# Delta net: products with V of both value heads interleaved over the four quarters of TensorE's array

## Chip, core and metric

One Trainium2 chip, one of its cores. The metric is the device time of the whole kernel in microseconds (us). The engines are called as the profile calls them: PE (TensorE's matmuls), PEld (its weight loads), DVE (VectorE), ACT (ScalarE), POOL (GpSimd) and SP (the queue that issues the DMAs).

## What is computed

A small perceiver-like model of six residual layers on x of 16 x 64 x 256 in float32: latent cross attention, attention, a feed-forward layer, a second cross attention, a gated delta net (`_L1_attn_ref`), and a mixture of experts. Only the delta net is touched. Cut to its core:

```
mixed = silu(conv4(hidden @ W_qkv.T))        # q, k: 16 heads of 128; v: 32 heads of 128
q, k = repeat(q, 2), repeat(k, 2)            # two value heads share one key head
q, k = l2norm(q) * DK**-0.5, l2norm(k)
g, beta = -exp(A_log) * softplus(a + dt_bias), sigmoid(b)
def step(state, (qt, kt, vt, gt, bt)):       # over the 64 positions
    state = state * exp(gt)
    delta = (vt - kt @ state) * bt
    state = state + outer(kt, delta)
    return state, qt @ state
o = rmsnorm(outs) * norm_w * silu(z)
y = o @ W_out.T
```

## The kernel before

Tokens lie as (2 batches x 64 positions) on 128 partitions, 8 such tiles (`TILES`). The delta net runs a loop over the 16 key heads; each brings two value heads (`hv` 0 and 1). The recurrence is written as matrices of 64 x 64 per batch and value head: `AT` (what is to be inverted), `T` (the inverse), `PT` (scores with decays), their product mixed, `Ms`, and then `Ms` times `V`. Since one batch needs 64 rows and 64 columns only, each product of this kind uses one quarter of the 128 x 128 array: batch 0 rows and columns 0 to 63, batch 1 rows and columns 64 to 127. The other two quarters are not used by them.

The order on every engine is written by hand in a function `step(j)` for that engine, and the engines meet at semaphores. In step j the kernel finishes head j while it projects and prepares head h = j + 1 (its convolution, its scores, its `AT`) and projects the output of head g = j - 1. These parts carry names that the prediction uses:

- `cross(j, 4)` on PE is the first use of `T` of head j. It waits for the DMAs that bring the inverted 16 x 16 blocks into `T` and `TT16` (the trace calls the wait "DMA TT<-t_blocks").
- After it PE runs two projections (`project`), `grow`, `scores(h)`, `turn_T`, `cross(j, 5)`, `grow(j, 5)` and the first projection of z (`project_z(j, 0)`). ACT takes tanh of that (`tanh_z`, tile `thz`), DVE multiplies (`silu_z`, tile `z2`), and only behind it in DVE's order stands `make_A(h, .)`, which writes `AT` of head h.
- SP waits for `AT` (`blocks_out(h)`), writes it to DRAM (`a_rows`), reads the blocks on the diagonal back as `sy`; POOL inverts them in 30 small dependent steps (`substitute`, tiles `tm`, `ti`); SP writes the result (`t_blocks`) and reads it back into `T` and `TT16` (`blocks_in`). That ends in `cross(h, 4)` of the next step.
- Meanwhile PE runs `mix(j, hv)` (T times PT into banks 4 and 5), DVE scales it to `Ms` (`keep_M`, with `sk`, one factor for each row), PE runs `project_z` 2 and 3, `outs(j, hv)` (`Ms` times `V` into banks 6, 7 for head 0 and 4, 5 for head 1), and then the output projection `project_out(g, .)`, `turn_v(h, 0)`, and the beginning of the next step, up to `cross(h, 4)`.
- `square_o` on ACT, and `gate`, `sum_o` and then `residual(g, .)` on DVE take up the results. `residual(g, 0)` frees banks 2 and 3, on which `turn_v(h, 0)` waits.
- `keep_v(h, hv)` on ACT copies `V` of one value head from PSUM into SBUF.

Of the kernel before, what the change touches and what calls it, by code (L numbers as in the profile page):

```python
# [6 lines left out]
ALU = mybir.AluOpType  # L7
ACT = mybir.ActivationFunctionType
AX = mybir.AxisListType

P = 128
B, S, D = 16, 64, 256
TILES = B * S // P
# [880 lines left out]
def phase3(nc, d, sb, semaphores, C, over, each, X, HT, PS, carrier):  # L894
# [9 lines left out]
    with ExitStack() as ctx:  # L904
        ga = sb(ctx, "ga", [P, TILES, 2 * HV])

        with ExitStack() as c2:
# [5 lines left out]
            s = semaphores(c2, "ab_in ab_mm ab_v ab_a")  # L913
            av, bv = ab[:, :, 0:HV], ab[:, :, HV:2 * HV]
            ea, eb = e[:, :, 0:HV], e[:, :, HV:2 * HV]
            with nc.Block() as block:
# [36 lines left out]
                def _(a):  # L953
# [23 lines left out]
        wo = sb(ctx, "wo", [P, 2, D])  # L977
# [15 lines left out]
        rr = sb(ctx, "rr", [P, 2, 2 * TILES])  # L993
        r2 = sb(ctx, "r2", [P, 2, 2 * TILES])
        sk = sb(ctx, "sk", [P, 2, TILES])
        dd = sb(ctx, "dd", [P, 2, TILES])
        AT = sb(ctx, "AT", [P, 2, 2, TILES, S])
        PT = sb(ctx, "PT", [P, 2, 2, TILES, S])
# [3 lines left out]
        T = sb(ctx, "T", [P, 2, TILES, S])  # L1002
# [3 lines left out]
        Ms = sb(ctx, "Ms", [P, 2, TILES, S])  # L1006
        V = sb(ctx, "V", [P, 2, TILES, DK])
        dl = sb(ctx, "dl", [P, 2, TILES, DK])
        ms = sb(ctx, "ms", [P, 2, TILES])
        s = semaphores(ctx, "win vin zin cin oin nin nws pj tap conv th y zz zt z2 qq kk dg nr nm rr gj gm dps e ed et av pd "  # L1010
                            "d1 sin sub d3 t16 tt tts x xs yy tu mt mss o us ms gz fz og0 og1 ogt ogs wo xa wof vt vc zero", "p3_")
        NQ = 8
        NS = 2 * SUB
        QB = (0, 1, 0, 1, 0, 1, 0, 0)
# [3 lines left out]
        def wide(b0):  # L1018
            return PS[:, b0:b0 + 2, :].rearrange("p k n -> p (k n)")

        def bank(k):
            return PS[:, k, :].rearrange("p (n s) -> p n s", s=S)
# [4 lines left out]
        def obank(hv):  # L1027
            return 6 if hv == 0 else 4
# [16 lines left out]
        def flat(ap):  # L1045
            return ap.rearrange("p n c -> p (n c)")

        with nc.Block() as block:
# [91 lines left out]
            def _(pe):  # L1140
# [81 lines left out]
                        mm = pe.transpose(PS[:, 2 + n // 4, (n % 4) * P:(n % 4 + 1) * P], y[:, 2 + hv, n * P:(n + 1) * P], C("ident"))  # L1222
                    mm.then_inc(s["vt"], 1)

                def each_batch(b0, lhs, rhs):

                    w = rhs.shape[2]
                    for n in range(TILES):
                        for b in range(2):
                            r = slice(64 * b, 64 * b + S)  # L1230
                            at = n * w
                            mm = pe.matmul(PS[r, b0 + at // 512, at % 512:at % 512 + w], lhs[r, n, :], rhs[r, n, :], start=True, stop=True)
                    return mm

                def turn_T(j, hv):
                    if hv == 0:
                        pe.wait_ge(s["tu"], j * 2 + 1)
# [41 lines left out]
                def mix(j, hv):  # L1279
                    if hv == 0:  # L1280
                        pe.wait_ge(s["tu"], j * 2 + 2)
                    pe.wait_ge(s["pd"], j * 2 + hv + 1)
                    each_batch(4 + hv, T[:, hv, :, :], PT[:, j % 2, hv, :, :]).then_inc(s["mt"], 1)

                def outs(j, hv):
                    pe.wait_ge(s["mss"], j * 2 + hv + 1)
                    pe.wait_ge(s["vc"], j * 2 + hv + 1)
                    each_batch(obank(hv), Ms[:, hv, :, :], V[:, hv, :, :]).then_inc(s["o"], 1)

                def turn_out(g, hv):  # L1290
                    pe.wait_ge(s[f"og{hv}"], g + 1)
# [29 lines left out]
                def step(j):  # L1321
                    h, g = j + 1, j - 1
                    beside, tail = h < HK, g >= 0
                    if beside:
                        project(h, 0)
                    turn_v(j, 1)
                    if beside:
                        project(h, 1)
                        decay_sums(h)
                        project(h, 2)  # L1330
                    if tail:
                        turn_out(g, 0)
                    if beside:
                        project(h, 3)
                    if tail:
                        turn_out(g, 1)
                    cross(j, 4)
                    if beside:
                        project(h, 4)
                    grow(j, 4)  # L1340
                    if beside:
                        project(h, 5)
                        scores(h)
                    turn_T(j, 0)
                    turn_T(j, 1)
                    cross(j, 5)
                    if beside:
                        project(h, 6)
                    grow(j, 5)
                    project_z(j, 0)  # L1350
                    if beside:
                        project(h, 7)
                    project_z(j, 1)
                    for hv in range(2):
                        mix(j, hv)
                    project_z(j, 2)
                    project_z(j, 3)
                    for hv in range(2):
                        outs(j, hv)
                    if tail:  # L1360
                        for m in range(4):
                            project_out(g, m)
                    if beside:
                        turn_v(h, 0)
# [15 lines left out]
            def _(a):  # L1380
                def tap(h, q):
                    c, f = q // 2, q % 2
                    if q == 0:
                        a.wait_ge(s["cin"], h * 16 + 16)
                    a.wait_ge(s["pj"], h * NQ + q + 1)
                    if h * NQ + q >= 2:
                        a.wait_ge(s["y"], h * NQ + q - 1)
                    a.activation(acc[:, f, :], PS[:, QB[q], :], ACT.Copy, scale=wc[:, h % 2, 4 * c + 3:4 * c + 4]).then_inc(s["tap"], 1)  # L1388

                def tanh(h, q):  # L1390
                    a.wait_ge(s["conv"], h * 24 + q * 3 + 3)
                    a.activation(th[:, q % 2, :], acc[:, q % 2, :], ACT.Tanh, scale=0.5).then_inc(s["th"], 1)  # L1392

                def tanh_z(j, m):
                    a.wait_ge(s["zz"], j * 4 + m + 1)
                    if j * 4 + m >= 2:
                        a.wait_ge(s["z2"], j * 4 + m - 1)
                    a.activation(thz[:, m % 2, :], PS[:, ZB[m], :], ACT.Tanh, scale=0.5).then_inc(s["zt"], 1)
# [27 lines left out]
                def keep_v(h, hv):  # L1426
                    a.wait_ge(s["vt"], h * 2 + hv + 1)
                    if h > 0:
                        a.wait_ge(s["o"], h * 2 - 2 + hv + 1)
                    a.activation(flat(V[:, hv, :, :]), wide(2), ACT.Copy).then_inc(s["vc"], 1)  # L1430

                def scale_wo(g):
                    a.wait_ge(s["oin"], g * 16 + 16)
# [8 lines left out]
                def step(j):  # L1442
                    h, g = j + 1, j - 1
                    beside, tail = h < HK, g >= 0
                    if beside:
                        tap(h, 0)
                    keep_v(j, 1)
                    if beside:
                        tap(h, 1)
                        tanh(h, 0)  # L1450
                        decays(h)
                        tap(h, 2)
                        tanh(h, 1)
                    if tail:
                        keep_out(g, 0)
                    if beside:
                        tap(h, 3)
                        tanh(h, 2)
                    if tail:
                        keep_out(g, 1)  # L1460
                    keep_X(j, 4)
                    if beside:
                        tanh(h, 3)
                        tap(h, 4)
                        tap(h, 5)
                        tanh(h, 4)
                    for hv in range(2):
                        keep_TT(j, hv)
                    if beside:
                        tanh(h, 5)  # L1470
                    keep_X(j, 5)
                    if tail:
                        scale_wo(g)
                    if beside:
                        tap(h, 6)
                        tanh(h, 6)
                    tanh_z(j, 0)
                    if beside:
                        tap(h, 7)
                    tanh_z(j, 1)  # L1480
                    if beside:
                        tanh(h, 7)
                    tanh_z(j, 2)
                    tanh_z(j, 3)
                    for hv in range(2):
                        square_o(j, hv)
                    if beside:
                        keep_v(h, 0)
# [4 lines left out]
                for q in range(NQ):  # L1493
                    tap(0, q)
                    if q == 3:
                        decays(0)
                    tanh(0, q)
                keep_v(0, 0)
                for j in range(HK):
                    step(j)  # L1500
                scale_wo(LAST)
# [91 lines left out]
            def _(v):  # L1593
# [56 lines left out]

                def keep_M(j, hv):
                    v.wait_ge(s["mt"], j * 2 + hv + 1)
                    v.tensor_tensor(Ms[:, hv, :, :], bank(4 + hv), each(sk[:, j % 2, :], S), ALU.mult).then_inc(s["mss"], 1)

                def residual(g, m):
                    v.wait_ge(s["wo"], g * 2 + m + 1)
# [298 lines left out]
```

## Time and profile before

| | |
|---|---|
| median of 3 runs | 1953.88 us (1947.71 to 1959.5) |
| the profiled execution: its own time / its span | 1954.76 us / 1952.6 us |
| mean granted clock of TensorE | 0.941 |
| the delta net's loop over heads | about 694 to 1643 us of the span |
| PE, POOL, DVE, ACT busy in the span | 88%, 28%, 60%, 31% |

The span is the time from the first to the last instruction; the profiled execution's own time has 2.2 us around it. A value of 1.00 in the column PEclk stands for the array at 2.4 GHz, 0.50 for 1.2 GHz; a value between them is a mean over a stretch that held both.

### The profile page before, as it was taken

How to read it: one execution, taken by the hardware profiler on the slowest of the kernel's cores; microseconds unless marked ns; L12 is line 12 of the kernel's file. 1: busy time of each engine (PE TensorE's matmuls, PEld its weight loads, DVE VectorE, ACT ScalarE, POOL GpSimd, SP SyncE). 2: the span in 40 equal slices, each digit the busy share in tenths (PEclk: the TensorE clock that was granted, in tenths of full speed). 3: DMA queues.
4: the chain of work that ended last, by engine and by line, in shares of the span. 5: the costliest groups of instructions: out<-in, count | busy, mean ns of one | idle time of the engine just before them, and what ended most of it. 6: DMA issues, size and time to landing. Idle time of an engine off the chain costs nothing. (4 is left out here: it accounts for less than half of the span.)

```text
span 1952.6 us, 34931 instructions
## 1 busy us (share of the span) xinstructions
PE 1719.2 (88%) x14360; PEld 1174.4 (60%) x14360; DVE 1164.5 (60%) x1853; ACT 600.8 (31%) x997; POOL 552.0 (28%) x890
## 2 busy tenths in 40 slices
PE   3899968998995548999999999999999877999998
PEld 1333336886784226766776777766677665556555
DVE  4555557678764537676777767776677613443432
ACT  1111114334422313343444333433433311212212
POOL 1100014113211045444445554453554321000000
PEclk9899978999997869999999999998999978999999
DMA  6221120010000111111122111211211113200000
GB/s 200 84 59 47 49 52 1 1 33 12 1 1 3 33 30 31 43 37 39 37 48 47 39 42 36 48 41 35 47 36 43 26 23 113 87 0 0 0 0 21
DMA packets 150907, 74.47 MB, mean 38 GB/s; under 512 B 128176, under 2 KB 131504, under 8 KB 149488
## 3 DMA queue, kind: packets, MB, share of 16 engines
q1 hardware_dynamic: 150768, 72.48, 14.5%
q8 instruction: 104, 1.70, 0.4%
q14 instruction: 35, 0.29, 0.1%
HBM read 54.62 MB, written 17.83 MB: 37 GB/s over the span
## 5 line engine op out<-in xcount | busy, mean ns | idle before, releaser
L1604 DVE SCALAR_TENSOR_TENSOR acc<-PS,wc,acc 128x504 f32<-128x504 f32 (+2 forms) x384 | 281.5, 733 | 104.7 <-ACT acc L1388 95.5
L1158 PE MATMUL PS<-HT,wv 128*128 128x512 f32 x256 | 140.5, 676 | 8.3 <-DVE acc L1604 8.3
L1528 POOL TENSOR_TENSOR rr<-nm,con 128x16 f32<-128x16 f32 x16 | 46.4, 2901 | 341.1 <-DVE nm L1632 341.1
L1175 PE MATMUL PS<-wz,HT 128*128 128x256 f32 x512 | 123.6, 390 | 18.4 <-DVE acc L1604 17.0
L1388 ACT ACTIVATE acc<-PS,wc 128x512 f32<-128x512 f32 x128 | 87.7, 685 | 168.0 <-PE PS L1158 119.3
L1158 PE MATMUL PS<-HT,wkq 128*128 128x512 f32 x256 | 125.1, 614 | 11.4 <-DMA wkq<-in_gdn_w 8.5
L1614 DVE SCALAR_TENSOR_TENSOR y<-th,acc 128x512 f32<-128x512 f32 x128 | 93.3, 729 | 60.6 <-ACT th L1392 60.4
L1175 PEld LDWEIGHTS PS<-wz,HT 128*128 128x128 f32 x512 | 95.1, 192 | 40.8 <-DVE acc L1604 19.0
L1316 PE MATMUL PS<-wo,ogT 128*128 128x256 f32 x512 | 116.9, 387 | 1.1 <-ACT ogT L1440 1.1
L298 PE MATMUL PS<-HT,cw 128*96 128x512 f32 x256 | 117.5, 613 | 0.0
L1392 ACT ACTIVATE th<-acc 128x512 f32<-128x512 f32 x128 | 80.2, 626 | 116.8 <-DVE acc L1604 116.6
L1260 PE MATMUL PS<-T,AT 64*64 64x32 f32 x2048 | 74.5, 232 | 43.7 <-DMA TT<-t_blocks 43.7
L1316 PEld LDWEIGHTS PS<-wo,ogT 128*128 128x128 f32 x512 | 97.6, 193 | 17.0 <-issue 2.6
L1260 PEld LDWEIGHTS PS<-T,AT 64*64 64x64 f32 x2048 | 71.7, 150 | 48.2 <-DMA TT<-t_blocks 48.0
L1790 PE MATMUL PS<-wg,hT 128*128 128x512 f32 x192 | 97.1, 631 | 0.6 <-DMA wu<-in_moe_u 0.3
L1808 PE MATMUL PS<-wd,acT 128*128 128x256 f32 x384 | 90.3, 382 | 2.2 <-ACT acT L1831 2.2
L1790 PE MATMUL PS<-wu,hT 128*128 128x512 f32 x192 | 90.3, 593 | 0.0
L1556 POOL TENSOR_TENSOR tm<-sy,ti 128x15 f32<-128x15 f32 (+7 forms) x240 | 63.8, 266 | 93.2 <-DMA sy<-a_rows 75.7
L298 PEld LDWEIGHTS PS<-HT,cw 128*96 128x96 f32 x256 | 41.6, 168 | 76.0 <-issue 76.0
L1877 DVE SCALAR_TENSOR_TENSOR act<-th,PS 128x512 f32<-128x512 f32 x48 | 33.0, 687 | 90.6 <-ACT th L1827 90.6
L1275 PEld LDWEIGHTS PS<-Xs,TT 64*64 64x64 f32 x2048 | 67.3, 144 | 29.3 <-issue 15.9
L370 DVE TENSOR_TENSOR ra<-PS,con 96x512 f32<-96x512 f32 x32 | 21.8, 683 | 101.7 <-PE PS L298 101.7
(228 smaller groups left out, 3357.6 us busy)
## 6 DMA issues: line engine op xcount, KB each, us to landing
a_rows<-AT SPq DMA_DIRECT2D x16, 512.0 KB, 2.6
wk<-in_l0x_k SPq DMA_DIRECT2D x16, 384.0 KB, 3.3
queries_scratch<-tts SPq DMA_DIRECT2D x32, 128.0 KB, 2.7
b<-queries_scratch SPq DMA_DIRECT2D x8, 512.0 KB, 5.0
wkq<-in_gdn_w SPq DMA_DIRECT2D x16, 256.0 KB, 3.2
wv<-in_gdn_w SPq DMA_DIRECT2D x16, 256.0 KB, 2.8
wz<-in_gdn_w SPq DMA_DIRECT2D x16, 256.0 KB, 2.9
wo<-in_gdn_w SPq DMA_DIRECT2D x16, 256.0 KB, 2.6
```

The source lines that it names most:

```text
L298: mm = pe.matmul(PS[0:HQ, 2 + 2 * f + c, :], cw[:, p, k, c * HQ:(c + 1) * HQ], HT[:, k, f * 512:(f + 1) * 512], start=(k == 0), stop=(k == ...
L1158: mm = pe.matmul(PS[:, QB[q], :], w[:, o:o + DK], HT[:, k, f * 512:(f + 1) * 512], start=(k == 0), stop=(k == DC - 1))
L1175: mm = pe.matmul(PS[:, ZB[m], w * 256:(w + 1) * 256], HT[:, k, n * P:(n + 1) * P], wz[:, k * 2 * DK:(k + 1) * 2 * DK], start=(k == 0), sto ...
L1260: mm = pe.matmul(PS[r, 6, m * 2 * SUB:(m + 1) * 2 * SUB], matrices(AT[r, j % 2, :, :, :])[:, m, :], cols, start=True, stop=True)
L1275: mm = pe.matmul(PS[r, 7, m * 2 * SUB:(m + 1) * 2 * SUB], matrices(turned[r, :, :, :])[:, m, :], Xs[r, m, :], start=True, stop=True)
L1316: mm = pe.matmul(PS[:, wbank(m), w * D:(w + 1) * D], ogT[:, hv, n * P:(n + 1) * P], wo[:, hv, :], start=(hv == 0), stop=(hv == 1))
L1388: a.activation(acc[:, f, :], PS[:, QB[q], :], ACT.Copy, scale=wc[:, h % 2, 4 * c + 3:4 * c + 4]).then_inc(s["tap"], 1)
L1392: a.activation(th[:, q % 2, :], acc[:, q % 2, :], ACT.Tanh, scale=0.5).then_inc(s["th"], 1)
L1604: v.scalar_tensor_tensor(a0, p0, wc[:, h % 2, 4 * c + 2 - k:4 * c + 3 - k], a0, ALU.mult, ALU.add).then_inc(s["conv"], 1)
L1614: v.scalar_tensor_tensor(y[:, c, f * 512:(f + 1) * 512], th[:, f, :], 1.0, acc[:, f, :], ALU.add, ALU.mult).then_inc(s["y"], 1)
L1790: mm = pe.matmul(PS[:, 4 * p + 2 * (m % 2) + o, :], hT[:, p, k, :], w[:, k, m * 512:(m + 1) * 512], start=(k == 0), stop=(k == DC - 1))
L1808: mm = pe.matmul(PS[:, 4 * p + 2, 0:D], acT[:, p, c * P:(c + 1) * P], wd[:, c, :], start=(c == 0), stop=(c == MC - 1))
```

## The change

`outs` now makes the products of both value heads in one loop, in the order batch 0 head 0, batch 0 head 1, batch 1 head 0, batch 1 head 1, so that they go round all four quarters of the array. For this `Ms` and `V` of value head 1 lie with their halves of 64 partitions swapped: `mix(j, 1)` writes its products to the other half of the columns, `keep_v(., 1)` copies V in two half copies to the other partitions, and `keep_M` of head 1 takes its factors from `skx`, a swapped copy of `sk` that ACT makes with two small copies a head (`swap_scale`). `outs` waits for both heads' `Ms` and `V` before its first product. The number of products stays what it was.

```
+        skx = sb(ctx, "skx", [P, 2, TILES])
...
-                    each_batch(4 + hv, T[:, hv, :, :], PT[:, j % 2, hv, :, :]).then_inc(s["mt"], 1)
-
-                def outs(j, hv):
-                    pe.wait_ge(s["mss"], j * 2 + hv + 1)
-                    pe.wait_ge(s["vc"], j * 2 + hv + 1)
-                    each_batch(obank(hv), Ms[:, hv, :, :], V[:, hv, :, :]).then_inc(s["o"], 1)
+                    for n in range(TILES):
+                        for b in range(2):
+                            r = slice(64 * b, 64 * b + S)
+                            w = r if hv == 0 else slice(64 * (1 - b), 64 * (1 - b) + S)
+                            mm = pe.matmul(PS[w, 4 + hv, n * S:(n + 1) * S], T[r, hv, n, :], PT[r, j % 2, hv, n, :], start=True, stop=True)
+                    mm.then_inc(s["mt"], 1)
+
+                def outs(j):
+
+                    pe.wait_ge(s["mss"], j * 2 + 2)
+                    pe.wait_ge(s["vc"], j * 2 + 2)
+                    for n in range(TILES):
+                        for b in range(2):
+                            for hv in range(2):
+                                w = slice(64 * b, 64 * b + S)
+                                r = w if hv == 0 else slice(64 * (1 - b), 64 * (1 - b) + S)
+                                mm = pe.matmul(PS[w, obank(hv) + n // 4, (n % 4) * P:(n % 4 + 1) * P], Ms[r, hv, n, :], V[r, hv, n, :],
+                                               start=True, stop=True)
+                                if n == TILES - 1 and b == 1:
+                                    mm.then_inc(s["o"], 1)
...
-                    a.activation(flat(V[:, hv, :, :]), wide(2), ACT.Copy).then_inc(s["vc"], 1)
+                    if hv == 0:
+                        a.activation(flat(V[:, 0, :, :]), wide(2), ACT.Copy).then_inc(s["vc"], 1)
+                    else:
+                        a.activation(flat(V[64:P, 1, :, :]), wide(2)[0:64, :], ACT.Copy)
+                        a.activation(flat(V[0:64, 1, :, :]), wide(2)[64:P, :], ACT.Copy).then_inc(s["vc"], 1)
+
+                def swap_scale(h):
+
+                    a.wait_ge(s["rr"], h * 5 + 3)
+                    if h > 1:
+                        a.wait_ge(s["mss"], h * 2 - 2)
+                    a.activation(skx[64:P, h % 2, :], sk[0:64, h % 2, :], ACT.Copy)
+                    a.activation(skx[0:64, h % 2, :], sk[64:P, h % 2, :], ACT.Copy).then_inc(s["sx"], 1)
...
                     if beside:
                         tap(h, 6)
                         tanh(h, 6)
+                        swap_scale(h)
                     tanh_z(j, 0)
...
+                    if hv == 1:
+                        v.wait_ge(s["sx"], j + 1)
+                    scale = (sk, skx)[hv]
+                    v.tensor_tensor(Ms[:, hv, :, :], bank(4 + hv), each(scale[:, j % 2, :], S), ALU.mult).then_inc(s["mss"], 1)
```

The order changes on ACT at two places, and on no other engine (on PE the 32 products of `outs` keep their place behind `project_z`, in another order among themselves). The first place is the middle of a step on ACT, from the copy of `Xs` to the second `thz`: before,

```order
L1418 ACTIVATE Xs<-PS,con 128x512
L1434 ACTIVATE wo<-wo,nw 128x512
L1388 ACTIVATE acc<-PS,wc 128x512
L1392 ACTIVATE th<-acc 128x512
L1398 ACTIVATE thz<-PS 128x512
L1388 ACTIVATE acc<-PS,wc 128x512
L1398 ACTIVATE thz<-PS 128x512
```

and of the changed kernel (its line numbers are 4 to 16 higher there):

```order
L1422 ACTIVATE Xs<-PS,con 128x512
L1450 ACTIVATE wo<-wo,nw 128x512
L1392 ACTIVATE acc<-PS,wc 128x512
L1396 ACTIVATE th<-acc 128x512
L1445 ACTIVATE skx<-sk 64x8
L1446 ACTIVATE skx<-sk 64x8
L1402 ACTIVATE thz<-PS 128x512
L1392 ACTIVATE acc<-PS,wc 128x512
L1402 ACTIVATE thz<-PS 128x512
```

Two small copies now stand ahead of the first `thz` of the step. The second place is the end of one step and the start of the next on ACT, where `V` is copied: before,

```order
L1424 ACTIVATE so<-PS 128x1024 x2
L1430 ACTIVATE V<-PS 128x1024
L1388 ACTIVATE acc<-PS,wc 128x512
L1430 ACTIVATE V<-PS 128x1024
L1388 ACTIVATE acc<-PS,wc 128x512
L1392 ACTIVATE th<-acc 128x512
```

and of the changed kernel:

```order
L1428 ACTIVATE so<-PS 128x1024 x2
L1435 ACTIVATE V<-PS 128x1024
L1392 ACTIVATE acc<-PS,wc 128x512
L1437 ACTIVATE V<-PS 64x1024
L1438 ACTIVATE V<-PS 64x1024
L1392 ACTIVATE acc<-PS,wc 128x512
L1396 ACTIVATE th<-acc 128x512
```

The second copy of V is made in two halves of 64 partitions, ahead of the second `acc` of the step.

## Rows read from the trace of the kernel before

**Rows 1.** The waits of the loop (750 to 1620 us): us, times, longest.

```profile
PE PS L1260 <- DMA TT<-t_blocks: 25.8, 14, 3.7
```

**Rows 2.** PE's timeline: start, us, line, count, [idle before <-releaser].

```profile
1019.64 1.92 PE L1208 MATMUL PS<-y 128*64 128x128 f32 x32
1021.87 2.08 PE L1245 MATMUL PS<-con,T 64*64 64x64 f32 x64 [0.31 <-DVE dg L1624]
1023.75 2.04 PE L1260 MATMUL PS<-T,AT 64*64 64x32 f32 x64
1025.72 1.98 PE L1158 MATMUL PS<-HT,wv 128*128 128x512 f32 x4
...
1041.85 3.71 PE L1232 MATMUL PS<-V,Ms 64*64 64x128 f32 x64
1045.49 7.17 PE L1316 MATMUL PS<-wo,ogT 128*128 128x256 f32 x32
1052.50 1.04 PE L1222 MATMUL PS<-con,y 128*128 128x128 f32 x8
1053.37 1.88 PE L1158 MATMUL PS<-HT,wkq 128*128 128x512 f32 x4
...
1065.77 2.06 PE L1260 MATMUL PS<-T,AT 64*64 64x32 f32 x64 [1.02 <-DMA TT<-t_blocks]
```

**Rows 3.** SP's timeline of the same step, DMA issues.

```profile
1034.19 0.33 SPq L1073 DMA_DIRECT2D a_rows<-AT  x1
1037.00 3.79 SPq L1081 DMA_DIRECT2D sy<-a_rows  x8
...
1052.69 0.35 SPq L1065 DMA_DIRECT2D wo<-in_gdn_w  x1
1053.49 0.33 SPq L1087 DMA_DIRECT2D t_blocks<-ti  x1
```

**Rows 4.** POOL's timeline of the same step, first and last of 32 instructions.

```profile
1042.39 0.21 POOL L1556 TENSOR_TENSOR tm<-sy,ti 128x15 f32<-128x15 f32 x1 [3.96 <-DMA sy<-a_rows]
...
1052.83 0.64 POOL L1560 COPY ti<-ti 128x256 f32<-128x256 f32 x1
```

**Rows 5.** DVE's timeline of the same step.

```profile
1032.28 0.69 DVE L1619 SCALAR_TENSOR_TENSOR z<-thz,PS 128x512 f32<-128x512 f32 x1 [0.92 <-ACT thz L1398]
...
1049.93 1.22 DVE L1657 TENSOR_TENSOR X<-X,PS 128x1024 f32<-128x1024 f32 x1
```

**Rows 6.** ACT's timeline of the same step.

```profile
1031.65 0.60 ACT L1398 ACTIVATE thz<-PS 128x512 f32<-128x512 f32 x1 [0.22 <-PE PS L1175]
...
1043.86 1.02 ACT L1424 ACTIVATE so<-PS 128x1024 f32<-128x1024 f32 x1 [1.31 <-PE PS L1232]
...
1056.16 1.02 ACT L1430 ACTIVATE V<-PS 128x1024 f32<-128x1024 f32 x1
```

**Rows 7.** One line's instructions: a small copy on ACT, ns min/median/max.

```profile
L956 ACT ACTIVATE al<-al x1: 213/213/213, 638.5 to 638.5; 128x32 f32<-128x32 f32 x1
```

**Rows 8.** PE's timeline at four `cross(j, 4)` of other steps.

```profile
839.28 2.33 PE L1260 MATMUL PS<-T,AT 64*64 64x32 f32 x64 [1.65 <-DMA TT<-t_blocks]
...
898.52 3.34 PE L1260 MATMUL PS<-T,AT 64*64 64x32 f32 x64 [3.73 <-DMA TT<-t_blocks]
...
956.10 2.06 PE L1260 MATMUL PS<-T,AT 64*64 64x32 f32 x64 [0.52 <-DMA TT<-t_blocks]
...
1288.70 2.06 PE L1260 MATMUL PS<-T,AT 64*64 64x32 f32 x64 [1.32 <-DMA TT<-t_blocks]
```

**Rows 9.** Stretches `cross(j, 4)` to DMA a_rows: us, busy (x) by engine, PEclk, DMA.

```profile
839.28:864.24 24.96, 24.65 (x413) 18.39 (x414) 16.88 (x26) 10.05 (x17) 10.04 (x13) 0.93 0.07 21
898.52:925.03 26.51, 26.19 (x413) 19.48 (x414) 15.40 (x24) 8.86 (x15) 10.04 (x13) 0.87 0.07 20
956.10:979.44 23.34, 23.03 (x413) 17.64 (x414) 17.09 (x26) 11.08 (x18) 10.04 (x13) 1.00 0.07 22
...
1344.87:1374.21 29.34, 29.34 (x413) 21.29 (x414) 16.91 (x26) 9.78 (x17) 9.72 (x12) 0.77 0.06 18
...
sum 322.16, PE 318.42 PEld 239.78 DVE 218.12 ACT 131.71 POOL 128.60; mean PE 24.49 PEld 18.44 DVE 16.78 ACT 10.13 POOL 9.89
```

More of the change, by code:

```diff
@@ L1010, in phase3 @@
         s = semaphores(ctx, "win vin zin cin oin nin nws pj tap conv th y zz zt z2 qq kk dg nr nm rr gj gm dps e ed et av pd "
-                            "d1 sin sub d3 t16 tt tts x xs yy tu mt mss o us ms gz fz og0 og1 ogt ogs wo xa wof vt vc zero", "p3_")
+                            "d1 sin sub d3 t16 tt tts x xs yy tu mt mss o us ms gz fz og0 og1 ogt ogs wo xa wof vt vc zero sx", "p3_")
         NQ = 8
@@ L1223, in turn_v @@
                     mm.then_inc(s["vt"], 1)
[L1225 to L1233, printed above, removed]
                 def turn_T(j, hv):
@@ L1357, in step @@
                     project_z(j, 3)
-                    for hv in range(2):
-                        outs(j, hv)
+                    outs(j)
                     if tail:
@@ L1498, in _ @@
                 keep_v(0, 0)
+                swap_scale(0)
                 for j in range(HK):
@@ L1652, in keep_M @@
                     v.wait_ge(s["mt"], j * 2 + hv + 1)
-                    v.tensor_tensor(Ms[:, hv, :, :], bank(4 + hv), each(sk[:, j % 2, :], S), ALU.mult).then_inc(s["mss"], 1)
+                    if hv == 1:
+                        v.wait_ge(s["sx"], j + 1)
+                    scale = (sk, skx)[hv]
+                    v.tensor_tensor(Ms[:, hv, :, :], bank(4 + hv), each(scale[:, j % 2, :], S), ALU.mult).then_inc(s["mss"], 1)
                 def residual(g, m):
```

## The prediction

> **What bounds the kernel now.** I read the list of waits first, because PE is busy nearly all the time in the delta net and the share of busy time says nothing about which wait ends last. One wait of PE stands out: 14 times, once for almost every head, PE stands still at the first `cross` for the DMAs that bring the inverted blocks, 25.8 us in all, 1.84 us a time [rows 1]. So in each step PE arrives too early at that place, and what ends the step is not PE.
>
> Then I read the timelines of one step to see what does. The DMA of `AT` is issued at 1034.19 and the blocks come back at 1037.0 and after; POOL inverts them from 1042.39 to 1053.47; `t_blocks` is issued at 1053.49, 0.02 us behind POOL; and `cross` starts at 1065.77 [rows 2 to 4]. These 31.58 us hold no work of PE at all. `outs` (1041.85 to 1045.49) lies beside them [rows 2]. The stretch before, from `cross` to the issue of `a_rows`, is PE's: at full clock it takes 23.34 us, of which PE is busy 23.03 [rows 9]. At its end `thz` starts when PE's z projection is done, DVE's multiplication follows it at 1032.28, and then `AT` [rows 5, 6]. A step is thus the sum of the two: 23.3 us of PE up to `AT`, and 31 to 34 us of DMA and POOL (from 864.24 to 898.52 in the longest) [rows 8, 9]. `outs` belongs to neither.
>
> The third view is the granted clock by stretches. Of the 13 stretches from a `cross` to the next `a_rows`, seven show clock 1.00 and 23.33 or 23.34 us; six were longer: 24.96 and 24.98, three times 26.51, and 29.34, with clock 0.93, 0.87 and 0.77 [rows 9]. In them the array ran at 1.2 GHz for a part. Together they cost 322.16 - 13 x 23.335 = 18.8 us, 3.1 us for each of the six. What came before tells them apart: the six follow waits at `cross` of 1.65 us (the shortest of them) to 3.73 us, the seven follow waits of 0.52 to 1.32 us [rows 8, 9]. No stretch breaks this order.
>
> **The change part by part.** *The products with V.* They are 64 instructions (two passes for each of 32 products) in 1045.49 - 1041.85 = 3.64 us, 57 ns each [rows 2]. A full-array instruction with the same 128 columns of data in one pass takes (1053.37 - 1052.50) / 8 = 109 ns, so two quarters already run side by side. With four the data side alone would give 27 ns, but there is a floor: 64-column instructions of the same quarters start (1023.75 - 1021.87) / 64 = 29 ns apart, and 32-column ones, with half the data, (1025.72 - 1023.75) / 64 = 31 ns apart [rows 2]. I take 31 ns: 64 x 31 = 1.97 us, a saving of 1.67 us a head. The other end is no saving at all, if two products in the same rows do not overlap.
>
> On that the trace has a row: `scores` uses all rows and alternates between the two halves of the columns, and its 32 instructions of 128 columns take 1.92 us, 60 ns each instead of 109 [rows 2]. Products that share rows but not columns do overlap. The Trainium skill (TensorE: Matmul & The Clock Gate, section on packing small matmuls) says that weight loads overlap with running matmuls only when the row group differs; by that the second and third product of each round of four would not overlap, and `outs` would stay near 3.64 us. The trace of `scores` disagrees with it, so I keep 1.97 us.
>
> *Where the saving goes.* PE begins `project_out` 1.67 us earlier and ends it at 1050.83 instead of 1052.50. There `turn_v` needs the banks that DVE's first residual frees. That one starts at 1049.93 because DVE's gates come first, and they start behind `square_o` of head 0. This head's result was ready after half of `outs` (1.82 us), and now comes at its end (1.97 us), so this chain is some 0.15 us later: 1049.93 + 1.22 + 0.15 = 1051.3 [rows 5, 6]. So `turn_v` starts near 1051.35, 1.15 us earlier than now, with a new wait of 0.5 us ahead of it. From there to `cross` nothing else holds PE back, and the 1.15 us are added to the wait at `cross`: waits of 0.52 to 3.73 us become 1.67 to 4.9 us. The chain over DMA and POOL has not moved, so the direct gain is nothing in every step with a `cross` behind it. In the last step the output of the head goes through the same `square_o` and gates, 0.15 us later. Direct gain: 0.
>
> *The half copies of V.* A half copy of 64 partitions has the same 1024 columns, so I price it as the whole: 1.02 us more on ACT a head [rows 6]. It delays the second `acc` of the step. PE and ACT are by then 1.15 us earlier than the wait at `cross` needs, and PE needs the convolution only later: hidden. Without that cover up to 1.0 us a step would show, and ACT would be late with `acc`, DVE with the convolution, PE with `project(h, 3)`.
>
> *The small copies ahead of `thz`.* These stand on the path that ends the step, as `thz` leads to `AT`. ACT has 0.22 us free there [rows 6], and a small copy takes 0.21 us at most [rows 7]. Two of them take 0.2 to 0.4 us, as far as they overlap, so they end 0 to 0.2 us after `thz` could have started. I take 0.05 us x 14 = 0.7 us; the ends are 0 and 3 us. Their source, `sk`, is ready long before. `mix(j, 1)` has the same number of products, in other quarters: 0. The added waits of `outs` are for an `Ms` done 2 us earlier: 0.
>
> *The clock.* This is the large term. Seven stretches now run at full clock after waits of 0.52 to 1.32 us; all seven waits become 1.67 to 2.5 us, at or above the 1.65 us from which every wait so far was followed by a stretch at half clock [rows 8, 9]. If that holds, each costs between 1.6 us and 6.0 us, 3.1 us in the mean, since the stretch is PE's own and lies on the path. Some waits will be only just above the bound, so I take five of the seven: 5 x 3.1 = 15.7 us. For the six that have it already I add nothing; more idle time may lengthen or shorten them.
>
> Sum: 0 + 0.7 + 15.7 = 16.4 us on the profiled execution's 1954.76 us: 1971 us. That execution stands 0.9 us from the median of the runs, so nothing has to be corrected.
>
> **The rivals.** *A: the wait grows, the clock does not fall more often.* For it: 1.65 us is one case, and what decides may be something other than the length of the wait. Against it: 13 stretches out of 13 are ordered by it. Time: 1954.8 + 0.7 = 1955.5, up to 1958 with the other end of the small copies. *B: `outs` does not get shorter,* because the quarters in the same rows do not overlap (the rule weighed above). Then no wait changes, and the time is again 1955 to 1958. Against it speaks `scores`. *C, on the other side: the half clock begins earlier, within the wait.* In a wait of 3 to 5 us the clock may fall while PE still stands idle, and be back sooner after it. The place is the same stretch behind `cross`; it decides if all stretches together lose less than 9 us instead of the present 18.8 us. With the loss halved and no new ones the time is 1955.5 - 9.4 = 1946; with none at all 1937. Against it: the 3.73 us wait, the longest, still cost 26.51 - 23.34 = 3.2 us [rows 8, 9]. *D: worse than forecast:* all seven and the longer form, 7 x 6.0 = 42 us, 1997.
>
> **How the numbers follow.** The forecast case has 0.58, A 0.18, B 0.08, C 0.12, D 0.04. Predicted is the likeliest, 1971 us. A measurement of this kernel can tell about 0.5% from no change, 9.8 us, so slower begins at 1963.7 and faster ends at 1944.1. The forecast case runs from three new stretches of 3.1 (1965) to seven and some longer (1985); a few of its outcomes fall under the bound, with two new stretches or short ones. Slower: 0.58 less 0.04, plus D: 0.58. Within 0.5%: A, B, these 0.04 and a third of C: 0.34. Faster: the rest of C, 0.08. The range of 8 in 10 takes in A and B at the low end, 1953, and leaves out most of C; at the top it reaches 1987 and leaves out D.
>
> **What the profile of the changed kernel would show.** `outs` as one group of 64 instructions in about 2.0 us (B: 3.6). A short wait ahead of the first transposes of V, for DVE's residual. The wait at `cross` near 3 us in the mean instead of 1.84. The small copies of 64 x 8 before `thz`, and `thz` moved by 0.2 us at most. POOL and SP spaced as before. The stretches from `cross` to `a_rows` mostly at 26.5 us with clock 0.87, where seven of 13 had 23.34. The forecast is wrong if the waits grow to 2 us and more and the clock stays at 1.00 behind them, or if a wait for ACT's V copies shows up on PE.

## The result

The changed kernel takes 1967.01 us (median of 22 runs, 1955.89 to 1980.66), the kernel before 1953.52 us (22 runs, 1947.71 to 1962.51). The ratio is 1.0062, 95% interval 1.0043 to 1.0080: some 12 us slower. The profiled execution has a span of 1970.6 us, against 1952.6 us before.

The products with V themselves became much faster. PE's timeline of one step of the changed kernel shows them (start, us, line, count, idle before and its releaser):

```profile
1168.14 1.98 PE L1290 MATMUL PS<-V,Ms 64*64 64x128 f32 x64
1170.05 7.17 PE L1321 MATMUL PS<-wo,ogT 128*128 128x256 f32 x32
1177.52 1.06 PE L1223 MATMUL PS<-con,y 128*128 128x128 f32 x8 [0.30 <-DVE X L1678]
```

From the first product to the start of the next group are 1.91 us, where before there were 3.64 [rows 2]. Behind the output projection stands the new wait for DVE's residual, 0.30 us.

The list of waits of the changed kernel, 750 to 1620 us (us, times, longest), shows where the time went:

```profile
PE PS L1251 <- DMA TT<-t_blocks: 37.6, 15, 4.5
...
PE PS L1223 <- DVE X L1678: 4.9, 14, 0.4
```

The wait at `cross(j, 4)` was 25.8 us in 14 times [rows 1], 1.84 us a time; it is now 37.6 us in 15 times, 2.51 us a time. SP's timeline of a step shows the other side, the chain over DMA and POOL:

```profile
1160.48 0.33 SPq L1074 DMA_DIRECT2D a_rows<-AT  x1
1164.04 3.76 SPq L1082 DMA_DIRECT2D sy<-a_rows  x8
...
1177.25 0.35 SPq L1066 DMA_DIRECT2D wo<-in_gdn_w  x1
1180.43 0.33 SPq L1088 DMA_DIRECT2D t_blocks<-ti  x1
1182.44 3.76 SPq L1095 DMA_DIRECT2D T<-t_blocks  x8
```

`cross` follows at 1192.07, 31.59 us behind `a_rows`; it was 31.58 us in the step shown of before [rows 2, 3]. The sum is the same, its parts are not. From `a_rows` to `t_blocks` it is 19.95 us here and was 19.30 us; from `t_blocks` to the first DMA that reads it back into `T` it is 2.01 us here and was 2.42 us:

```profile
1055.91 3.76 SPq L1094 DMA_DIRECT2D T<-t_blocks  x8
```

One part of this chain does hang on PE. On SP the load of `wo` stands just ahead of `t_blocks`, and it waits for PE's output projection: that ends at 1045.49 + 7.17 = 1052.66 before, and SP issues the load at 1052.69 [rows 2, 3]; now it ends at 1170.05 + 7.17 = 1177.22, and the load is issued at 1177.25. `t_blocks` then follows 0.80 us behind the load before, and 3.18 us behind it now.

ACT's timeline of the same step holds the two small copies, and `thz` directly behind them, with no idle time left between them:

```profile
1157.63 0.21 ACT L1445 ACTIVATE skx<-sk 64x8 f32<-64x8 f32 x1
1157.85 0.21 ACT L1446 ACTIVATE skx<-sk 64x8 f32<-64x8 f32 x1
1157.96 0.57 ACT L1402 ACTIVATE thz<-PS 128x512 f32<-128x512 f32 x1
```

The stretches from `cross(j, 4)` to `a_rows` of the changed kernel (us, busy by engine, granted clock PEclk, DMA) answer to [rows 9]:

```profile
841.45:872.11 30.66, 30.54 (x413) 22.17 (x414) 16.11 (x25) 9.32 (x18) 10.15 (x13) 0.74 0.06 16
905.99:936.79 30.80, 30.68 (x413) 22.32 (x414) 15.71 (x25) 9.04 (x17) 10.14 (x13) 0.74 0.05 14
968.81:995.43 26.62, 26.31 (x413) 19.46 (x414) 16.78 (x26) 10.25 (x19) 10.15 (x13) 0.87 0.07 20
1026.20:1051.27 25.07, 24.76 (x413) 18.38 (x414) 17.09 (x26) 10.90 (x20) 10.14 (x13) 0.93 0.07 19
1082.37:1105.81 23.44, 23.13 (x413) 17.61 (x414) 17.15 (x27) 11.29 (x20) 10.15 (x13) 1.00 0.08 23
...
1414.69:1445.44 30.75, 30.63 (x413) 22.26 (x414) 16.52 (x26) 9.78 (x18) 10.15 (x13) 0.74 0.06 17
1477.23:1507.00 29.77, 29.64 (x413) 21.28 (x414) 17.18 (x26) 10.53 (x20) 10.15 (x13) 0.77 0.06 19
...
sum 344.17, PE 340.89 PEld 253.15 DVE 217.19 ACT 135.50 POOL 130.22; mean PE 26.22 PEld 19.47 DVE 16.71 ACT 10.42 POOL 10.02
```

PE executes the same 413 instructions in each, so the length follows the granted clock. Those at full clock take 23.44 us instead of 23.34: the small copies. There are five of these (seven before), and four of the eight others take 29.8 to 30.8 us, where before one of six took over 29 us. The 13 stretches sum to 344.17 us against 322.16: 22.0 us more, 1.4 us by the small copies (13 x 23.44 against 13 x 23.335) and 20.6 us by the clock.

Over the same 13 steps the time from `a_rows` to `cross` fell by 6.1 us in sum (from 419.6 to 413.5 us, 741.76 - 322.16 and 757.63 - 344.17). It lies between the issue of `t_blocks` and the first DMA that reads it back: 33.7 us in sum before, 26.7 us now. The earlier load of `wo` accounts for a part. In all twelve profiles this time is 2.02 us in the median where `wo` was issued over 2 us ahead of `t_blocks` (92 steps), and 3.09 us where it was under 1 us (36 steps). Before, eight of the 13 steps had under 1.5 us and took 2.6 us in sum above 2.02 us each; two others took 4.21 and 3.83 us, for which the trace shows no reason. No run moved the load, so this is read from times alone.

So this execution is 15.9 us longer there, of 18.0 us in all.

### The profile page after: what moved, and what is told of

Its sections match the earlier page's. It is cut to its first block and busy times, and to the rows that moved or that the text cites. A ratio compares the mean times of both kernels' runs of the same rounds, so it can differ in the third digit from the quotient of the medians.

```text
span 1970.6 us, 34993 instructions
## 1 busy us (share of the span) xinstructions
PE 1715.5 (87%) x14360; PEld 1155.2 (59%) x14360; DVE 1167.3 (59%) x1853; ACT 618.4 (31%) x1045; POOL 552.0 (28%) x890
## 5 line engine op out<-in xcount | busy, mean ns | idle before, releaser
L1159 PE MATMUL PS<-HT,wv 128*128 128x512 f32 x256 | 151.0, 720 | 8.3 <-DVE acc L1622 8.3
L1632 DVE SCALAR_TENSOR_TENSOR y<-th,acc 128x512 f32<-128x512 f32 x128 | 97.6, 762 | 71.0 <-ACT th L1396 70.6
L1266 PEld LDWEIGHTS PS<-Xs,TT 64*64 64x64 f32 x2048 | 72.3, 152 | 31.7 <-issue 18.1
L1159 PEld LDWEIGHTS PS<-HT,wv 128*128 128x128 f32 x256 | 51.8, 220 | 53.4 <-issue 39.7
```

The lines of the kernel that those rows point to most:

```text
L1159: mm = pe.matmul(PS[:, QB[q], :], w[:, o:o + DK], HT[:, k, f * 512:(f + 1) * 512], start=(k == 0), stop=(k == DC - 1))
L1266: mm = pe.matmul(PS[r, 7, m * 2 * SUB:(m + 1) * 2 * SUB], matrices(turned[r, :, :, :])[:, m, :], Xs[r, m, :], start=True, stop=True)
L1632: v.scalar_tensor_tensor(y[:, c, f * 512:(f + 1) * 512], th[:, f, :], 1.0, acc[:, f, :], ALU.add, ALU.mult).then_inc(s["y"], 1)
```

## The experiments

The theory: a step is the sum of PE's stretch up to `AT` and of a chain over DMA and POOL in which PE has no part. What `outs` saves becomes idle time ahead of `cross(j, 4)`, and idle time there makes the array's clock fall more often behind it, where PE does set the pace. (This theory leaves out the load of `wo`, the one place of the chain that hangs on PE.) The main rival: the swapping costs the time (the copies on ACT, the other quarters in `mix`). All ratios are to the kernel before on the same chip, whose median was 1945.5, 1946.1 and 1942.3 us in the three groups of runs. Since each kernel has one profile, the mean granted clock of all its executions stands here first:

```
kernel                              executions   mean granted clock
before (three groups)               23, 18, 16   0.942, 0.941, 0.942
changed (first group, k12)          22, 11       0.930, 0.931
k1_swap_only                        12           0.942
k2_half_outs                        6            0.925
k3_fill_after                       12           0.943
k4_fill_before                      12           0.9435
k9_moved                            7            0.929
k5_early, k6_early_before           6, 6         0.936, 0.942
k10_early_fill, k11_before_...      6, 6         0.946, 0.947
```

A longer part of the time at half clock lowers this mean; work added or left out moves it a little as well.

**The changed kernel without the interleaving** (`k1_swap_only`). All swapping stays.

```
+                    for hv in range(2):
+                        for n in range(TILES):
+                            for b in range(2):
-                    for n in range(TILES):
-                        for b in range(2):
-                            for hv in range(2):
```

> The changed kernel with all its swapping (half copies of V, skx, mix of head 1 in the other quarters, one common wait), but outs makes the products of head 0 and then those of head 1, so only two quarters run side by side. Theory (the saved 1.1 us a step becomes idle time ahead of cross(j, 4), and the clock falls more often behind it; the small copies cost 0.1 us a step): outs takes 3.6 us again, the waits at cross(j, 4) are 0.5 to 3.7 us again, about half of the stretches behind them run at full clock at 23.44 us, and the time is that of before plus 14 x 0.1 = 1.4 us: 1953 to 1957, ratio 1.000 to 1.002. Rival (the copies on ACT or the other quarters in mix cost the time): 1964 to 1969, ratio near 1.006.

Measured: 0.9976 (0.9952 to 1.0000). The swapping is not what costs the time, and the clock of its 12 executions is that of before. By the clock theory's own number it was to be 0.1% above before, and it is at or a little below it. The waits of its profile (same columns as above):

```profile
PE PS L1251 <- DMA TT<-t_blocks: 22.4, 15, 3.5
```

`outs` takes 3.27 us here, not 3.64: where the products of head 1 follow those of head 0 all four quarters are in use for a moment (22 instructions in half a microsecond at that place, 14 elsewhere). Of 14 stretches three ran at half clock for a part; 13 of them lose 6.5 us to the clock (18.8 us before).

**The kernel before, with half of the products with V left out** (`k2_half_outs`). The output is not the reference's: tiles 4 to 7 have no products.

```
-                    each_batch(obank(hv), Ms[:, hv, :, :], V[:, hv, :, :]).then_inc(s["o"], 1)
+                    for n in range(TILES // 2):
+                        for b in range(2):
+                            r = slice(64 * b, 64 * b + S)
+                            mm = pe.matmul(PS[r, obank(hv), n * P:(n + 1) * P], Ms[r, hv, n, :], V[r, hv, n, :], start=True, stop=True)
+                    mm.then_inc(s["o"], 1)
```

> The kernel before, with the products of outs for the first 4 of the 8 tiles only (half of the products with V is left out; nothing else is changed, no swapping). PE has 1.8 us less work a step, at the same place where the change saves 1.7 us. Theory: less work makes the kernel slower, by as much as the change does, ratio 1.003 to 1.009, with waits at cross(j, 4) longer by some 1.1 us and more stretches behind them at half clock. Rival (the swapping costs the time, or PE's work is on the path): ratio 1.000, or below it by up to 25 us (0.987).

Measured: 1.0100 (1.0082 to 1.0119), a little more than the theory's upper end. This is the plainest of the runs: nothing is swapped, nothing added, PE has 1.7 us less to do in each step, and the kernel is 19 us slower, with a clock of 0.925 in the mean of its six executions. Its waits and three of 13 of its stretches with their sum:

```profile
PE PS L1260 <- DMA TT<-t_blocks: 37.0, 15, 3.6
```

```profile
1071.59:1097.71 26.12, 25.81 (x413) 19.67 (x414) 15.35 (x24) 8.87 (x15) 10.04 (x13) 0.88 0.07 21
1129.51:1152.84 23.33, 23.02 (x413) 17.63 (x414) 16.23 (x25) 9.36 (x16) 10.04 (x13) 1.00 0.08 25
...
1471.34:1501.67 30.33, 30.33 (x413) 22.28 (x414) 14.93 (x23) 8.66 (x15) 9.72 (x13) 0.74 0.06 18
...
sum 337.71, PE 333.99 PEld 250.77 DVE 210.68 ACT 125.41 POOL 128.57; mean PE 25.69 PEld 19.29 DVE 16.21 ACT 9.65 POOL 9.89
```

The waits are those of the changed kernel, and the stretches lose 337.71 - 13 x 23.33 = 34.4 us to the clock. For the changed kernel the same sum gives 344.17 - 13 x 23.44 = 39.5 us.

**Useless products ahead of the wait**, two in the changed kernel (`k3_fill_after`) and one in the kernel before (`k4_fill_before`).

```
                     if k == 4:
-                        pe.wait_ge(s["t16"], j * 256 + 256)
                         if j + 1 < HK:
                             pe.wait_ge(s["e"], j * 2 + 3)
                         else:
                             pe.wait_ge(s["xa"], j * 2 - 2)
+                        if j > 0:
+                            for _ in range(2):
+                                pe.matmul(PS[:, 6, :], C("ident"), HT[:, 0, 0:512], start=True, stop=True)
+                        pe.wait_ge(s["t16"], j * 256 + 256)
```

> The changed kernel with two products of 128x128 with 128x512 ahead of the wait of cross(j, 4), into bank 6, which cross overwrites: 1.7 us of useless work a step, while PE would stand idle for 0.9 to 4.5 us. Theory (the time is lost at half clock behind the idle time): the idle time falls to 0 to 2.8 us, fewer stretches run at half clock than in the kernel before (six of 13), and the time is 1940 to 1953, below the changed kernel's 1967 and at or below before's. Rival (the clock falls for another reason than this wait): no faster than the changed kernel, 1967 to 1975.

Measured: 0.9964 (0.9949 to 0.9980). 15 x 1.7 = 26 us of added work make the changed kernel about 1% faster than it is without (1.0062, and 1.0075 measured again below), and a little faster than before. Its 13 stretches lose 9.6 us to the clock instead of 39.5. The products fill idle time that cost more than itself. One step of its profile:

```profile
955.48 1.88 PE L1248 MATMUL PS<-HT,con 128*128 128x512 f32 x4
958.97 2.06 PE L1254 MATMUL PS<-T,AT 64*64 64x32 f32 x64 [1.61 <-DMA TT<-t_blocks]
```

The mean granted clock from 790 to 1580 us is 0.98 in this profile, 0.94 in that of the changed kernel and 0.97 in that of before.

> The kernel before with one useless product of 128x128 with 128x512 (0.86 us) ahead of the wait of cross(j, 4). Theory (the clock falls behind idle time, more often the longer it is): the idle times fall by 0.86 us, fewer stretches run at half clock, and added work makes also this kernel faster, or at least not slower: ratio 0.993 to 1.000. Rival (added work costs its time where the wait is shorter than 0.86 us, and the clock does not follow): 1.001 to 1.006.

Measured: 0.9994 (0.9979 to 1.0009). One product adds 13 us of work in all and costs nothing that can be measured. It lies within both the theory's range and its "at least not slower"; its interval ends just short of the rival's 1.001, so it speaks against the rival only weakly.

**The small copies moved off the path** (`k9_moved`), and the changed kernel once more beside it (`k12_changed_again`, in the next group of runs).

```
                         tanh(h, 6)
-                        swap_scale(h)
...
                     tanh_z(j, 2)
+                    if beside:
+                        swap_scale(h)
```

> The changed kernel with the two small copies (skx) behind the third thz instead of ahead of the first. Theory: each stretch from cross(j, 4) to a_rows is 0.10 us shorter, 23.34 us where the clock is full, 1.5 us in all; the waits and the clock stay as in the changed kernel, so that the ratio is 1.002 to 1.008. Rival (the small copies are more of the loss than that): ratio 1.000 or less.

> The changed kernel itself, for the ratio on the same chip beside the others. 1.004 to 1.009, with 1.1 us longer waits at cross(j, 4) and about two of three stretches with a part at half clock.

Measured: 1.0082 (1.0051 to 1.0114) with the copies moved, 1.0075 (1.0050 to 1.0100) for the changed kernel. The stretch at full clock is back at 23.33 us, as expected, and the time shows nothing of it: 1.5 us are less than these runs can tell, and the small copies are no part of the loss that matters. In `k12_changed_again` the waits at `cross` are 34.4 us in 15 times, and 11 of 14 stretches had a part at half clock, a little more than the two of three expected. Its 13 stretches lose 26.8 us to the clock, where the first profile of the same kernel loses 39.5: that is how far two executions of one kernel, on two chips, differ. This is one of the stretches of `k9_moved`:

```profile
1128.36:1151.69 23.33, 23.02 (x413) 17.62 (x414) 17.12 (x27) 10.99 (x18) 10.04 (x13) 1.00 0.08 24
```

**The path made shorter.** If a step is PE's stretch plus the chain, then `AT` should be written as early as it can be. On DVE it stood behind the multiplication with the first `thz`, for which it does not need to wait. `k5_early` makes this move in the changed kernel (with the small copies moved as above), `k6_early_before` in the kernel before.

```
-                    silu_z(j, 0)
                     if beside:
                         make_A(h, 0)
                         make_A(h, 1)
+                    silu_z(j, 0)
+                    if beside:
                         make_P(h, 0)
```

> The changed kernel with two moves that follow from where the path lies: DVE makes the two AT ahead of the multiplication with thz of z's first part instead of behind it, and the two small copies stand behind the third thz. Theory (the path of a step is PE's stretch up to AT and then DMA and POOL): AT is written some 1.5 us earlier, so the chain over DMA and POOL ends 1.5 us earlier relative to PE, the waits at cross(j, 4) are back to 0.5 us and more, and each of 14 steps is shorter by 1.4 us: 20 us off the changed kernel, more where the clock falls less often: 1935 to 1948. Rival (something else paces the steps): 1960 to 1970.

> The kernel before with only the DVE move: the two AT ahead of the multiplication with thz. It tells whether the four quarters are of use once the path is shorter. Theory: AT is written 1.6 us earlier, but PE has 1.1 us more work between AT and cross(j, 4) than in the changed kernel, so the waits of 0.5 to 3.7 us shrink to 0 to 2.1 us, PE is the bound in the calm steps, and the gain is 1.0 to 1.6 us a step less what PE then lacks, with less half clock: ratio 0.986 to 0.993. If the quarters matter it is slower than the changed kernel with the same move (0.990) by a step's shortfall of 0.1 to 0.5 us; if the fallen idle time counts for more it is as fast or faster.

Measured: 0.9898 (0.9866 to 0.9931) and 0.9931 (0.9904 to 0.9959). The stretch at full clock is 21.72 us in both (23.44 us in the changed kernel, 23.33 us in the one before). The theory's number for the first was met (0.9898 x 1953.5 = 1934 us, 1 us below the range); the second lies at the upper end of its range. The intervals overlap, so these two alone do not settle whether the quarters are of use now.

**Both together**, with one useless product, with the quarters (`k10_early_fill`) and without (`k11_before_early_fill`).

> The changed kernel with the DVE move, the small copies behind the third thz, and one useless product (0.86 us) ahead of the wait of cross(j, 4). Theory: the idle times of 0.2 to 3.2 us fall by up to 0.86 us and fewer stretches run at half clock, which gives some 5 to 8 us, and the steps with less than 0.86 us idle lose up to 0.6 us each: ratio 0.985 to 0.990, a little below the same kernel without it. Rival (the product costs more than the clock gives): 0.990 to 0.994.

> The kernel before with the DVE move and the useless product of 0.86 us, without the four quarters: the counterpart of the fastest kernel so far (0.9825). PE has 1.1 us more work between AT and cross(j, 4) than there, and the waits left to it after the DVE move are short. Theory (with the shorter path PE's work counts, so that the quarters now give something): 0.988 to 0.995, slower than 0.9825. Rival (the quarters never matter; the useless product and the move do it all): 0.980 to 0.985.

Measured: 0.9825 (0.9799 to 0.9851; 1908.1 us, against 1946.1 us before) and 0.9918 (0.9886 to 0.9950). The first is faster than both kernels, 1.8% below before, and beats its expectation. Here the quarters are worth 0.9%, and the two profiles show where. From `a_rows` to `cross` a step takes 31.69 us with the quarters and 32.90 us without, in the mean of 13. In six of the 13 steps of each kernel PE does not wait at `cross` at all, and this time is PE's own work: 31.25 to 31.50 us with the quarters, 32.48 to 32.66 us without. One such step of each (the `a_rows` and the `cross` behind it, `k10_early_fill` first):

```profile
1022.09 0.33 SPq L1074 DMA_DIRECT2D a_rows<-AT  x1
1053.38 2.06 PE L1254 MATMUL PS<-T,AT 64*64 64x32 f32 x64
```

```profile
1024.13 0.33 SPq L1073 DMA_DIRECT2D a_rows<-AT  x1
1056.61 2.06 PE L1263 MATMUL PS<-T,AT 64*64 64x32 f32 x64
```

In the other steps the chain sets the time, and it too is longer without the quarters: PE's output projection ends later, and the load of `wo` behind it comes closer to `t_blocks`. SP issues `wo` 0.39 to 1.0 us ahead of `t_blocks` there (1.32 to 2.48 us with the quarters), and the time from `t_blocks` to its first reader is 3.04 us in the mean of the 13 steps, against 2.17 us. In some steps `t_blocks` itself comes late, up to 0.99 us behind POOL. One step of `k11_before_early_fill` shows both; POOL's last instruction ahead of `t_blocks` ends at 1206.02:

```profile
1206.62 0.35 SPq L1065 DMA_DIRECT2D wo<-in_gdn_w  x1
1207.01 0.43 SPq L1087 DMA_DIRECT2D t_blocks<-ti  x1
1210.48 3.76 SPq L1094 DMA_DIRECT2D T<-t_blocks  x8
```

One step of `k10_early_fill` on PE and its stretch:

```profile
944.21 1.02 PE L1248 MATMUL PS<-HT,con 128*128 128x512 f32 x2
946.23 2.06 PE L1254 MATMUL PS<-T,AT 64*64 64x32 f32 x64 [0.99 <-DMA TT<-t_blocks]
...
1000.36 2.06 PE L1254 MATMUL PS<-T,AT 64*64 64x32 f32 x64 [1.00 <-DMA TT<-t_blocks]
```

```profile
946.23:967.96 21.73, 21.42 (x407) 16.56 (x408) 16.14 (x25) 9.31 (x16) 8.58 (x11) 1.00 0.08 24
```

The step takes 54.13 us, of which 32.40 are the chain over DMA and POOL. It bounds this step and six more of the 13; in the six without a wait PE's own work does.

**What idle time does to the clock.** Eight profiles (before, changed twice, k1, k2, k5, k6, k9) hold 109 pairs of a wait at `cross(j, 4)` of under 10 us and the stretch behind it. Counted by the length of the wait:

```
wait (us)      stretches   with a part at half clock
under 1.15        23            1
1.15 to 2.0       43           19
2.0 to 2.6        16           12
over 2.6          27           26
```

The bounds of the rows were not fixed ahead of the runs. The four kernels with useless products are left out; they have 32 such pairs, in which 5 of 22 stretches behind waits under 1.15 us and 5 of 10 behind 1.15 to 2.0 us had such a part. So the length of the wait does not decide alone. Behind a `cross` with no wait at all there were 27 stretches in the twelve profiles, and every one ran at full clock.

## Why the prediction was right, and where it was not

The median, 1967.0 us, lies within the range of 1953 to 1987 us, 4 us below the 1971 us named, and the direction was the one given 0.58. The mechanism, idle time that brings the half clock onto the path, is the one forecast. That the number is so close is in part luck: three terms were off, and their errors cancel. In the 13 steps of the profile the sum is 1.4 us by the small copies, 20.6 us by the clock and -6.1 us between `a_rows` and `cross`; predicted for the whole loop were 0.7, 15.7 and 0. Point by point:

- *`outs` at 1.97 us, saving 1.67 us.* It takes 1.91 us, 30 ns an instruction; the saving is 1.73 us. The row of `scores` was the right one to trust. The Trainium skill's rule on weight loads and row groups (TensorE: Matmul & The Clock Gate, section on packing small matmuls) would have left it near 3.6 us, rival B. The trace disagrees with it: four products that share rows or columns in pairs ran side by side here, at 30 ns an instruction.
- *The saving turns into idle time, less a new wait for the residual.* Predicted 0.5 us of wait and 1.15 us more idle at `cross`; measured 0.30 us of wait. PE arrives at `cross` 30.56 us behind `a_rows` before (1065.77 - 1.02 - 1034.19) and 29.31 us now (1192.07 - 2.28 - 1160.48, the 2.28 us being this step's wait). That is 1.25 us; in the mean of the 13 steps it is 1.03 us (30.42 and 29.39). Yet the wait grew by 0.56 us only (1.86 to 2.42), since the chain ended 0.47 us sooner. The prediction named a mean wait near 3 us instead of 1.84; it is 2.51.
- *The direct gain is 0.* Not so in this profile: 6.1 us came off the chain. "These 31.58 us hold no work of PE at all" was wrong, since SP's load of `wo`, just ahead of `t_blocks`, waits for PE's output projection. That explains a part of the 6.1 us; the rest is unexplained, and one profile of each kernel cannot show that it is the change. The term stays small beside the clock: `k1_swap_only` has an `outs` 1.36 us longer a step and is faster than the changed kernel.
- *The half copies of V: hidden.* PE waits for no half copy in the list of waits. Confirmed, also by `k1_swap_only`, which has them and is not slower than before.
- *The small copies: 0.05 us a step.* They cost 0.10 us in each stretch, 1.5 us in all, too little to be seen in the time.
- *The clock: five of seven calm stretches fall, at 3.1 us each.* Mechanism right, two sizes wrong. The count was too high: of the seven calm stretches three fell in the profile, for 11.2 us, and one of the six others came back to full clock. My statement that 1.65 us orders all stretches was an artefact of 13 cases: stretches behind waits of 1.66, 1.77, 1.91 and 2.28 us stayed at full clock here, and one behind 1.41 us did not. The table above shows no edge but a chance that climbs from 1 in 23 to 26 in 27 between 1.15 and 2.6 us. And for the six that had fallen already I had added nothing, but they cost 9.5 us more; the long form, 6.3 to 7.4 us, came in four of 13 stretches, behind waits of 2.39 to 4.54 us. The two errors go in opposite directions, and 20.6 us of clock in this profile stand against 15.7 us predicted. The profile is not the middle of the runs either: it took 1972.5 us, 5.5 us above the median, and the second profile of the same kernel lost 8.0 us more than before's to the clock instead of 20.6.
- *Rival A* (the wait grows, the clock is not touched) and *rival C* (the half clock moves into the idle time and costs less) are out: on one chip the changed kernel's mean clock is 0.931 over 11 executions against 0.942 over 16 of the kernel before, and `k2_half_outs` loses 34.4 us to the clock in 13 stretches, with waits like the changed kernel's. That the clock is what idle time costs is shown by runs in both directions, less work (slower) and useless work (faster).

What stays open: how much of the 6 us from `a_rows` to `cross` the earlier load of `wo` gives, and why `k1_swap_only` is at or slightly below the kernel before instead of 1.4 us above it. Its clock over all executions is the same, so it is not the clock; its profile has 28.1 us in sum from `t_blocks` to the first reader, against 33.7 us before, which would be about enough. Nothing was run for either. It was not tried either whether useless products at another place of the step would help as much as those just ahead of the wait.

## What to carry to other kernels

When an engine waits for the same thing in every round, time saved on it between the start of the awaited chain (here the write of `AT`) and that wait is not saved; shorten what lies ahead of the start. Before calling such a chain free of the engine, read the order on the DMA queue: a transfer that waits for the engine may stand in it, as the load of `wo` does here. On PE the saving may be worse than nothing, since here the array came out of longer waits at half clock more often, and then it is on the path: look at the granted clock of the stretch behind each wait before and after. Useless products just ahead of the wait are a cheap test of this, and were a gain of 1% here.

## What was not expected of the hardware

- No sharp length of idle time decides whether the clock falls. Waits of 1.83, 1.84 and 1.86 us were followed by full clock in some steps, and waits of 1.18 and 0.83 us by a part at half clock in others. The added lengths gather at 1.6 to 1.7, 2.7 to 3.2 and 6.0 to 7.4 us over the stretch at full clock (one of 58 was 4.0).
- Four quarters of the array in fp32, 64 x 64 with 128 columns of data, start an instruction every 30 ns, the same as two quarters with 64 or 32 columns (29 and 31 ns, [rows 2]); two quarters with 128 columns need 57 ns.
- Half copies on ACT of 64 partitions with 1024 elements take the time of the whole copy, 1.02 us (`V`, L1437 and L1438; the whole one in [rows 6]).
- A DMA of 256 KB issued just ahead of another one on the same queue goes with a later landing of the second: `t_blocks` took 3.09 us to its first reader in the median where `wo` was issued under 1 us ahead of it, 2.02 us where it was over 2 us. A few steps took up to 4.2 us with a longer lead, so this is not the only reason.
